# Half of each softmax weight multiply moved from VectorE to GpSimd in a transformer block's attention

## What is computed

```python
x = x + 0.5 * ffn(layernorm(x))
x = x + attn_block(layernorm(x))
x = x + 0.5 * ffn(layernorm(x))
```

```python
S = jnp.einsum('bthd,buhd->btuh', q, k)
S = S - dist_scale * abs(t - u)
S = jnp.where(mask_uh, -jnp.inf, S)     # key u, head h: masked where h > u
P = jax.nn.softmax(S / sqrt(64), axis=2)
A = jnp.einsum('btuh,buhd->bthd', P, v)
```

## Time and profile before

| what | value |
|---|---|
| two timed runs | 3761.56 and 4030.16 us, median 3895.86 |
| profiled execution | 3756.5 us |
| its span on the slowest core (core 7) | 3755.0 us |
| spans of all cores | 3746.9 to 3755.0 us |
| busy: PE, DVE, ACT, POOL | 2618.0, 1541.8, 1042.1, 222.8 us |
| attention, first scores to last write of L724 | 1084.19 to 2138.16 us |

### The profile page before, as it was taken

One profiled execution on the slowest core, in us unless ns is written; L12 is line 12 of the kernel. 1 busy time (PEld: TensorE's weight loads), 2 busy tenths in 40 slices (PEclk: granted clock), 3 DMA queues, 4 the chain that ended last, 5 costly groups with the idle time before them and its releaser, 6 DMA issues.

```text
span 3755.0 us, 34205 instructions; the slowest of 8 cores (3746.9 to 3755.0 us)
## 1 busy us (share of the span) xinstructions
PE 2618.0 (70%) x10819; PEld 1011.0 (27%) x10819; DVE 1541.8 (41%) x3256; ACT 1042.1 (28%) x1322; POOL 222.8 (6%) x117
## 2 busy tenths in 40 slices
PE   4309999963976666666566683958668521999997
PEld 2104444421421111111111131423223201444443
DVE  3553444453045455545555373011110254344445
ACT  0201111121325555555555413121212210111110
POOL 0210000012000000000000043010100130000000
PEclk9659999976987777777777695979789755999996
DMA  3022313114799800000000020625445301111002
GB/s 88 4 45 40 54 26 56 29 59 103 90 112 111 114 1 1 1 0 1 1 1 1 23 90 16 145 86 118 128 85 140 67 0 37 48 57 49 31 29 90
DMA packets 226665, 204.21 MB, mean 54 GB/s; under 512 B 148199, under 2 KB 199528, under 8 KB 223224
## 3 DMA queue, kind: packets, MB, share of 16 engines
q1 hardware_dynamic: 205996, 139.10, 13.7%
q0 software_dynamic: 20496, 62.93, 12.9%
HBM read 248.09 MB, written 52.51 MB: 80 GB/s over the span
## 4 chain that ended last, share of the span: by engine, by line
PE 58%; DVE 17%; ACT 10%; issue 7%; DMA 4%; POOL 2%; DVEq 1%; ACTq 0%; POOLq 0%; SPq 0%
PE pA L437 13%; PE pB L480 13%; PE pA L879 6%; ACT AR L674 5%; PE pB L910 5%; PE pB L649 5%; DVE AR L681 4%; PE pA L528 3%; PE pA L712 3%; PE pA L665 2%; PE pB L561 1%; DVE AR L293 1%; DVE AR L704 1%; POOL AR L287 1%; DVE AR L716 1%
## 5 line engine op out<-in xcount | busy, mean ns | idle before, releaser
L437 PE MATMUL pA<-AR 128*128 128x512 bf16 x2304 | 502.5, 381 | 8.2 <-DMA AR<-wcWs 8.2
L480 PE MATMUL pB<-AR 128*128 128x512 bf16 x2304 | 499.2, 379 | 0.3 <-DVE AR L461 0.3
L681 DVE TENSOR_TENSOR AR<-AR 128x512 bf16<-128x512 bf16 x1024 | 384.8, 418 | 242.6 <-ACT AR L674 224.0
L649 PE MATMUL pB<-AR 128*65 128x512 bf16 x1024 | 351.8, 429 | 163.4 <-DVE AR L691 83.7
L674 ACT ACTIVATE AR<-pA 128x1024 bf16<-128x1024 f32 x352 | 350.8, 1024 | 236.2 <-PE pA L665 233.9
L449 ACT ACTIVATE AR<-pA 128x512 bf16<-128x512 f32 x288 | 156.4, 595 | 803.0 <-PE pA L437 803.0
L879 PE MATMUL pA<-AR 128*128 128x512 bf16 x1024 | 232.7, 391 | 151.2 <-DMA AR<-wcW1a 99.5
L488 DVE SCALAR_TENSOR_TENSOR AR<-pB,AR 128x512 f32<-128x512 f32 x320 | 220.5, 691 | 260.0 <-PE pB L480 260.0
L437 PEld LDWEIGHTS pA<-AR 128*128 128x128 bf16 x2304 | 226.3, 98 | 282.6 <-issue 13.2
L480 PEld LDWEIGHTS pB<-AR 128*128 128x128 bf16 x2304 | 225.3, 98 | 272.7 <-issue 1.3
L712 PE MATMUL pA<-AR,onesrs 1*64 1x512 f32 x128 | 111.3, 966 | 204.5 <-ACT AR L709 204.5
(11 more groups left out here) (134 smaller groups left out, 2039.7 us busy)
## 6 DMA issues: line engine op xcount, KB each, us to landing
AR<-wcW1a SPq DMA_DIRECT2D x32, 1024.0 KB, 5.5
AR<-wcW2a SPq DMA_DIRECT2D x32, 1024.0 KB, 6.9
AR<-x SPq DMA_DIRECT2D x16, 512.0 KB, 3.6
AR<-W1e POOLq DMA_DIRECT2D x8, 1024.0 KB, 17.6
AR<-W2e POOLq DMA_DIRECT2D x8, 1024.0 KB, 13.0
AR<-probsp SPq DMA_DIRECT2D x16, 512.0 KB, 11.2
x1sp<-AR SPq DMA_DIRECT2D x8, 1024.0 KB, 3.9
wcW1a<-W1a POOLq DMA_DIRECT2D x1, 8192.0 KB, 89.6
```

Source lines behind the costliest of these rows:

```text
L437: lastmm = p.on("tensor", lambda e, j=j, dc=dc, fc=fc, tq=tq, ps=pp[f2]: e.matmul(ps, w1v[j][:, dc, 128 * fc:128 * (fc + 1)], xn(dc)[:, 51 ...
L480: lastmm = p.on("tensor", lambda e, j=j, fc=fc, do=do, tq=tq, ps=ps: e.matmul(ps, w2v[j][:, fc, 128 * do:128 * (do + 1)], h2s(j, fc, tq), ...
L649: last = p.on("tensor", lambda e, uc=uc, hh=hh, h=h: e.matmul(accs[hh][0:65, :], self.av_slice(uc, h), ptb[uc % 3][:, 512 * hh:512 * (hh + ...
L681: tv = p.on("vector", lambda e, sl=sl, off=off, hh=hh: e.tensor_tensor(ptb[sl][:, 512 * hh:512 * (hh + 1)], ebuf[sl][:, 512 * hh:512 * (hh ...
```

## The change

One of VectorE's two multiplies per tile of keys goes to GpSimd, for the first head of the pair. GpSimd's waits for the exponential and for the `ptb` slot, as VectorE's does. The matmuls with the values wait for both engines, and so does the exponential that reuses `ebuf`. The memset of the first head's masked partitions stays on VectorE and now waits for GpSimd's multiply also.

```diff
@@ emit_pv @@
-                            wait=[tv_done[uc], tok_v] +
+                            wait=[tv_done[uc], tg_done[uc], tok_v] +
                                  ([acc_free[hh]] if uc == 0 else []),
@@ for uc in range(NTC) @@
+                    ef = e_free[sl]
+                    ef = ef if isinstance(ef, list) else [ef]
                     te = p.on("scalar", lambda e, po=po, sl=sl: e.activation(
                         ebuf[sl], po, AF.Exp, bias=-12.0, scale=1.0),
-                        wait=[lastmm, e_free[sl]], inc="s")
+                        wait=[lastmm] + ef, inc="s")
                     slot_free[sl] = te
                     off = 1920 + 512 * tb - 128 * uc
-                    tv = None
-                    for hh in range(2):
-                        tv = p.on("vector", lambda e, sl=sl, off=off, hh=hh: e.tensor_tensor(
-                            ptb[sl][:, 512 * hh:512 * (hh + 1)],
-                            ebuf[sl][:, 512 * hh:512 * (hh + 1)],
-                            widb[:, off:off + 512], ALU.mult),
-                            wait=[te, pt_free[sl]] if hh == 0 else [],
-                            inc="v" if hh == 1 else None)
+                    tg_ = p.on("gpsimd", lambda e, sl=sl, off=off: e.tensor_tensor(
+                        ptb[sl][:, 0:512],
+                        ebuf[sl][:, 0:512],
+                        widb[:, off:off + 512], ALU.mult),
+                        wait=[te, pt_free[sl]], inc="g")
+                    tv = p.on("vector", lambda e, sl=sl, off=off: e.tensor_tensor(
+                        ptb[sl][:, 512:1024],
+                        ebuf[sl][:, 512:1024],
+                        widb[:, off:off + 512], ALU.mult),
+                        wait=[te, pt_free[sl]], inc="v")
                     if uc == 0:
                         if hA > 0:
                             tv = p.on("vector", lambda e, sl=sl, hA=hA: e.memset(
-                                ptb[sl][0:hA, 0:512], 0.0), wait=[tv], inc="v")
+                                ptb[sl][0:hA, 0:512], 0.0), wait=[tv, tg_], inc="v")
@@
-                    e_free[sl] = tv
+                    tg_done[uc] = tg_
+                    e_free[sl] = [tv, tg_]
```

More of the change, by code:

```diff
@@ L644, in attn_phase @@
                 tv_done = [None] * NTC
+                tg_done = [None] * NTC
                 def emit_pv(uc):
```

## The result

The changed kernel takes 1.0898 times the time of the one before, with a 95% interval of 1.0884 to 1.0912. The medians are 4101.6 and 3761.42 us, about 340 us more. The forecast of 4148 us had the direction, and the time lies in its range, but it had 390 us of loss where there are 340. Runs in which the cores of a die were held at a lower clock are left out of every ratio and of the times of single runs, but not of the medians; without them these are about 4098 and 3760 us, 338 us apart.

A forecast was written before the change was run, and what follows sets the result against it. TensorE paced the loop at the low clock, ScalarE was nearly full at full clock, and VectorE's half was latency. 3756.5 + 202.6 (stall) + 189 (loop) = 4148 us, range 4025 to 4255.

The forecast's parts named there:

- Part 1, the stall: Start of attention: the first multiply waits on POOL's queue behind six copies, from 1086.03 to 1288.64 us, +202.6 us.
- Part 2, POOL's time: Attention loop: one 128x512 multiply on POOL takes 1.27 us, from float32 rows, between 0.42 and 1.6.
- my case of a slower bf16: Rival, attention loop: a POOL multiply takes 1.6 us, pitch 1.78, +9.6 us a block, total 4266 us; chance 0.14.
- Part 3, the turns: Attention loop: POOL and VectorE multiplies alternate instead of overlapping; pitch 1.5 us a tile, +189 us over 32 blocks.
- the side-by-side rival: Attention loop: bf16 multiplies on POOL and VectorE overlap, 1.22 us a tile, total 4026 us; chance 0.14.
- the pitch of 1.69 with nothing saved: Rival, attention loop: no time saved at handover, or memsets take turns too; total 4235 us; chance 0.15.
- The ring of three: Attention loop: three score slots limit tiles to 1.3 to 1.5 us each, so turns bound or are just tied.
- A sign that misled: Attention loop: many VectorE multiplies would record above 1 us; staying at 0.42 beside running POOL would refute the prediction.
- the other side: Rival: POOL's multiplies pass the copies' waits, attention starts at 1086 and the loop falls to 1.02; 3722 us; chance 0.01.
- A block: One attention block: tile 0 is 0.8 us late, twelve more tiles at 1.5 us, +5.9 us in all.
- The end of a block: L704 to L724, after a block's tiles: no POOL work beside it, so given no price.
- VectorE's freed time: Attention: the half taken off VectorE gains nothing, since VectorE was already idle before the exponential.

The follow-up runs named there:

- experiment 1: Kernel before, with one of the 1024 multiplies (pair 0, block 0, tile 0, first head) moved to POOL: 1.0554 times before.
- experiment 2: Changed kernel with the six copies recorded inside attention, one at the start of every third block: 1.0354 times before, median 3894.5 us.
- experiment 3: Changed kernel with the six copies spread through attention and VectorE's second-head multiply left out: 3837.4 us in a single profiled run.
- experiment 4: Changed kernel with copies spread through attention and VectorE's second-head multiply replaced by a maximum of PSUM scores and table: 3846.1 us, single profiled run.
- experiment 5: Kernel before, with the first head's multiply left out and nothing in its place: 0.9815 times before, 70 us less.
- experiment 6: Changed kernel with copies spread through attention, POOL taking 128 of the first head's 512 columns and VectorE the other 384: 1.0148 times before.

## Why the prediction was right, and where it was off

- **Part 1, the stall: right.** 202.6 us were worked out from the issue of the last copy, 202.1 lie in the trace, and experiments 1 and 2 give 197 to 220 and 207. That nothing covers it is shown by both.
- **Part 2, POOL's time: the size was near, the row read too high.** I took 1.27 from float32 rows. In bf16 it is 1.11 start to start. The type makes little difference, and my case of a slower bf16 falls away. The prediction's estimate of 1.11 from the Trainium skill ("GPSIMD Engine Reference", section "Elementwise — side-by-side cycle accounting") was the better of the two for this bf16 multiply, though the page prices float32 only; the float32 pair of the earlier trace rows is 1.21 start to start, which the row of 1.27 had hidden. But the prediction's pitch from it, 1.41, takes the 0.12 off VectorE's turn only. Off both turns, as in its own 1.45, it is 0.99 + 0.30 = 1.29, a block +3.2 us and the total 4062. That the 4113 it gives lies nearest to the measured time is luck.
- **Part 3, the turns: right in kind, mis-sized.** They hold for bf16, by experiments 3 and 4, so the side-by-side rival falls, and the pitch of 1.69 with nothing saved falls too. **The term of the sum that was mis-sized is the pitch:** 1.5 where the trace has 1.30 at full clock. The way of adding the turns was nearly right. With the bf16 records of 1.15 and 0.42 it gives 1.03 + 0.30 = 1.33. So 0.12 of the miss is POOL's row, 0.03 the handover, and 0.05 what I added for the low clock. Counted start to start, VectorE's turn costs POOL 1.30 - 1.11 = 0.19 us. The ring of three is nearly tied with the turns, as the prediction allowed: VectorE's multiply, which waits for the same exponential, starts only 0.1 us before POOL is free. I had also let TensorE's 1.53 of the low clock pull the pitch up over the whole block. It holds for some four tiles only, as before: the granted clock of the block's second part is 0.90.
- **A sign that misled.** The prediction said that VectorE's multiplies would often be above 1 us in their record, and that it was wrong if they stayed at 0.42 beside a running POOL instruction. At full pace they do stay at 0.42 to 0.43 (1638.22, 1639.51), and the turns hold all the same. VectorE starts 0.1 us earlier, so POOL's record carries the wait. Its pitch of 1.45 to 1.55 and its blocks of 39 us were missed too: 1.30 and 37.2 on average.
- **The pitch before.** The 1.11 us a tile that the prediction gives to the full clock takes in one tile of the low clock. For tiles at the full clock alone it is 1.06 (exponentials at 1394.69 and 1397.86, three tiles apart). The sum doesn't use it, but two of the rivals do, side by side and the other side.
- **A block.** Tile 0 is 0.78 us late (1625.64 - 1622.53 against 1385.74 - 1383.41), where I had 0.8. From VectorE's first multiply to the last of the block it is 1646.16 - 1622.53 = 23.6 us against 19.6, so +4.0 where I had +5.9. By 32 that is 130 us for 189. The block isn't an odd one: 142.8 us of the table, less the 14 or 15 below for the ends, leaves 128 for the 32 loops.
- **The end of a block: costed at nothing, and it did cost something.** The prediction said that no POOL work lies beside it, which is so. But its spreading matmuls take 1.068 us on average (L718) where L712 took 0.966 before, 12.5 us in all. Over all blocks, from the first head's sum to the next block's first multiply it is 13.0 us on average where it was 12.5, 15 us in 32 blocks. First the group after, then the first pair of such a matmul in a block of the kernel before:

```profile
L718 PE MATMUL pA<-AR,onesrs 1*64 1x512 f32 x128 | 123.8, 1068 | 204.2 <-ACT AR L715 204.2
1406.11 1.04 PE L712 MATMUL pA<-AR,onesrs 1*64 1x512 f32 x2 [2.38 <-ACT AR L709]
```

It took 1.04 for the two there, and 1.93 in the block above (1649.28). The granted clock is 1.00 around the one (1405 to 1407.5) and 0.50 around the other (1648.5 to 1651.5): the 1.2 GHz level in place of 2.4. The second pair of a block ran at the lower level before, too. The loop ahead of it has more idle time of TensorE now; that this is why the clock falls sooner is argued, not tested. With these 12.5 us the 130 become the 142.8 of the table. The two misses, a loop priced too high and an end priced at nothing, partly cancel in the total.
- **Wo's load: rightly costed at nothing.** It was issued at 2472.91 and landed in 13.5 us instead of 23.4. Before, it was issued 0.6 us behind the last copy, and now no copy runs beside it. It was needed at 2505.78.
- **VectorE's freed time pays nothing: half right.** It was latency and not the pace, but worth 70 us if it had been free, since the loop's floor is 0.93 and not 1.02. The earlier trace rows could have told: two exponentials in 1.94 us are 0.92 start to start. The "other side" rival used the same wrong floor. By experiment 5 it would have ended some 35 us lower.

The loss, put together from the runs: 84 us (3846.1 - 3761.9) for POOL's multiply of 1.11 us where VectorE's two take 0.76, with nobody in its way, 48 for the turns, 207 for the stall. Together 339. That they meet the 340 measured is no proof, as each is the difference of one run to the next; the independent sum is that of experiments 1 and 2. The split between the first two rests on a single run of experiment 4, and on its trace.

## What to carry to other kernels

An instruction moved to another engine joins that engine's queue: look at what stands ahead of it there, above all DMA issues that wait for each other, before you look at its own time. Here one multiply of 1.16 us behind six copies cost about 200 us. Between GpSimd and VectorE, work on two on-chip operands was not shared out but lined up: price it as a sum of turns. And taking the turns away is not enough. With VectorE reading PSUM the move still lost 84 us here, as POOL takes 1.11 us for what took VectorE half of 0.76. And relieving an engine that sits idle for the one before it gives little (1.9% at the most here): find the chain that waits from engine to engine, as the block's end here, where a new order, with a row and an inverse for each head, gave 5%.

## What the runs showed that I had not expected

- The record of an exponential (1.02 us) is longer than its pace: back to back they start 0.93 apart. A multiply of VectorE, too, is 0.42 in the record, and two in 0.76 start 0.34 apart. For a floor, take start to start, and look whether a second engine stands at the same floor, as TensorE does here.
- Who carries the wait in the record changes. At full pace it was POOL (1.34 for 1.11), as VectorE's started 0.1 us earlier; for the 128 columns of experiment 6 both did (0.61 for 0.43, 0.65 for 0.42).
- POOL's 128x128 bf16 multiply takes 0.43 us and its 128x512 takes 1.11 to 1.15: as an estimate, a fixed part of about 0.2 us.
- A chain of copies that nobody waited for became the path for 330 us as soon as one instruction stood behind it, from 963 us on: the projections beside it are now off the path.
